# First gate product, weight sums, zero rows and residual loads moved in a one-core mixture kernel

## The chip, the cores and the metric

The kernel runs on one core of one Trainium2 chip. The time is the device time of one execution in microseconds (us), as the median of the runs shown.

## The reference

x has 32 sequences of 64 rows and 1024 columns in float32; taken together they are 2048 tokens. Two residual layers are computed:

```python
y = einsum('bct,bcd->bdt', x, W0[cond])            # a 64 x 64 matrix per sequence
x = x + y @ weight.T + lora(y, top-2 gates of y)    # 1024 -> 1024, 8 experts of rank 16
z = einsum('bsi,boi->bso', x, W1[adapter])          # a 1024 x 1024 matrix per sequence
gate, up = bitlinear(z, w_gate), bitlinear(z, w_up) # 1024 -> 2752
x = x + bitlinear(gate * up, w_down)                # 2752 -> 1024
# bitlinear(x, w): s = mean(|w|); q = round(clip(w / (s + 1e-5), -1, 1)); x @ (q * s).T
```

The three weights of the bitlinears are read once for the mean of their absolute values and again to be rounded to -1, 0 or 1.

## The kernel before

Every float32 operand of a product is split into a high and a low float16 part (act_t holds both for all tokens, 1024 columns on the partitions as 8 chunks). ScalarE writes the high part and VectorE the low part. The order of work on each engine is written out by hand; engines meet at semaphores (wait_ge), and an engine's instructions, the DMAs that it issues among them, go strictly in program order.

**First layer.** The 16 token tiles (NT) of 128 are mixed, gated and multiplied with the first weight; a tile's product is summed in PSUM pair t % 2 (pair[0] to pair[3] are 2-bank PSUM tensors of 1024 float32 columns), and VectorE's residual (L1566) adds x, which releases the pair (acc_released).

**Adapter products.** The sequences are sorted by adapter and paired into slots; there are between 16 and 20 slots, as the data decide, and the first 17 always have their instructions. linear (L854) is the product of a slot, 48 matmuls into pair k % 2. Its adapter rank and column are read into registers (slot_fields). copy_z takes the result out (ScalarE the left half, VectorE the right), linear_t transposes it on TensorE into pair 2 (L667), high_z (ScalarE) and low_z (VectorE) put it into act_t. The slots past FIRST_OPTIONAL = 17 stand in nested conditionals (optional).

Meanwhile GpSimd loads w_up and w_down in 24 pieces (load_piece, L631; six buffers), and VectorE sums the absolute values of each (sum_piece, L1621). The last four pieces are summed behind low_z of slot 12. When all are there, TensorE adds the sums over partitions in one product with ones (L922, into pair 3), and VectorE derives the clipping bounds and scales.

**Gate stage.** The 22 chunks (IC) of 128 inner columns go through a pipeline: load_q loads the natural rows of the three weights (SP queue), quantize (VectorE, L1656) clips them, round_q (ScalarE, L1202) rounds, turn_q (TensorE, L900) transposes, store_q (ScalarE, L1218) takes them into wa and wd, turn_a and turn_b (VectorE, L1679 to L1684, L1664 to L1669) form the sums of a seven-product (Strassen) scheme, which are stored to DRAM for later token groups (store_wa, store_wb). gate_up(n, s) (L946) is the product of chunk n with the first 512 tokens: 16 matmuls for the gate into pair 0, 16 for up into pair 1. scale_gate (ScalarE, L1235) and product (VectorE, L1700) multiply them; inter_sums (L1688 to L1693), high_inter (L1239) and low_inter (L1673) prepare the operand of the down stage. PE's order around its start is:

```python
            turn_q(1, 1, 0, (0, 1))
            linear_t(k - 2, 1)
            turn_q(1, 1, 0, (2,))
            optional(k, 1, pairs)
...
            gate_up(0, 0)
            pe.wait_ge(z_low, NSLOT)
            turn_q(2, 0, 1)
            gate_up(1, 1)
```

The last chunk has only 64 rows. VectorE waits until its tiles are free (q_turned), writes zeros into the other rows (L1653) and clips.

**Down stage and later token groups.** The tokens go in four groups of 512 (g = 0 to 3). down(g) (L1019) does seven products of 44 matmuls, each with one of seven weight sums, loaded into two alternating buffers by load_products (SP queue, L533; the load for product q waits until product q - 2 is done). The residual rows come by load_res (L545), four loads of 512 KB into the place of the inter sums st. From g = 1 on the gate and up products of a group come from the stored sums as well (unit, L982; loads L537), and GpSimd makes the low parts of the inter operand (L652) instead of VectorE. turn_t on VectorE (L1745 to L1756) prepares the next group's tokens during a down stage.

## Time and profile before

| what | value |
|---|---|
| median of 3 runs | 1394.69 us (1393.57 to 1394.8) |
| profiled execution, its own time | 1395.66 us |
| its span in the trace | 1394.0 us |
| TensorE busy (PE) | 1334.8 us, 96% |
| VectorE (DVE), ScalarE (ACT), GpSimd (POOL) busy | 54%, 27%, 11% |
| DMA | mean 223 GB/s |
| granted TensorE clock, mean | 0.986 of full |

The span is measured from the first to the last instruction of the profiled execution; its own time is 1.66 us longer. A matmul counts as busy with a modelled end, so two neighbouring rows overlap a little. In the rows, a bracket gives how long the engine was idle before the instruction and what released it; "issue" means that the trace shows nothing that it waited for. PEld is TensorE's weight load, SPq, ACTq and POOLq the queues of the engines that issue DMAs.

### The profile page before, as it was taken

To read this page: it belongs to the slowest core of one execution; us is meant where nothing else is said; L and a number is where in the kernel's file an instruction comes from. 1 tells how busy PE (TensorE), PEld (TensorE's weight loads), DVE (VectorE), ACT (ScalarE), POOL (GpSimd) and SP (SyncE) were. 2 spreads that over 40 slices of the span, in tenths; PEclk is the share of its full clock that TensorE was granted. 3 is DMA by queue.
4 is the path that set the end of the run, shared out by engine and by line. 5 is a ranking of instruction groups with operands and counts; after the bars stand their busy time and mean duration, and the time that the engine had idled before them with its cause. 6 is when DMAs were issued, how large, how long until landed. Compare 5 with 4: busy or idle time off the path is not lost.

```text
span 1394.0 us, 24489 instructions
## 1 busy us (share of the span) xinstructions
PE 1334.8 (96%) x8864; PEld 854.4 (61%) x8865; DVE 750.4 (54%) x1159; ACT 369.8 (27%) x401; POOL 157.5 (11%) x115
## 2 busy tenths in 40 slices
PE   5889899979999998999999999999999999999998
PEld 5874444434544454555544788854888844888843
DVE  4467555443355565888855355573455581455521
ACT  2423344100111145888730011120111110111100
POOL 3200000000111000000000122320133310222210
PEclk9999999989999999999999999999999999999999
DMA  8644999989997927999874644353634455544354
GB/s 211 161 137 176 337 408 416 331 261 221 295 265 236 271 95 265 360 350 358 291 264 166 219 159 149 139 202 138 228 141 153 148 194 185 204 158 155 128 196 143
DMA packets 174336, 310.67 MB, mean 223 GB/s; under 512 B 99360, under 2 KB 131360, under 8 KB 166464
## 3 DMA queue, kind: packets, MB, share of 16 engines
q1 hardware_dynamic: 158352, 254.04, 55.8%
q10 hardware_dynamic: 11440, 32.69, 6.2%
q0 software_dynamic: 4480, 23.07, 4.8%
q8 instruction: 41, 0.67, 0.2%
q14 instruction: 23, 0.19, 0.0%
HBM read 220.78 MB, written 68.03 MB: 207 GB/s over the span
## 4 chain that ended last, share of the span: by engine, by line
PE 73%; DMA 10%; DVE 5%; SPq 5%; issue 4%; ACT 2%; POOL 1%; POOLq 0%; ACTq 0%; DVEq 0%
PE pair L982 26%; PE pair L1019 15%; PE pair L854 12%; PE pair L946 10%; DMA region_q<-in_L_cond_weight 5%; PE pair L770 4%; DMA region_q<-wb_scratch 2%; PE pair L900 2%; DMA region_w<-in_L_ffn_w_gate 2%; SPq L474 2%; PE pair L737 1%; PE pair L667 1%; PE pair L725 1%; DMA region_q<-in_x 1%; SPq L445 1%
## 5 line engine op out<-in xcount | busy, mean ns | idle before, releaser
L982 PE MATMUL pair<-act_t,region_q 128*128 128x256 f16 x3696 | 404.0, 273 | 0.0
L982 PEld LDWEIGHTS pair<-act_t,region_q 128*128 128x128 f16 x3696 | 361.6, 98 | 42.5
L1019 PE MATMUL pair<-region_q,region_w 128*128 128x512 f16 x1232 | 267.6, 379 | 4.7 <-DMA region_q<-wb_scratch 4.4
L1019 PEld LDWEIGHTS pair<-region_q,region_w 128*128 128x128 f16 x1232 | 120.0, 98 | 151.0 <-DMA region_q<-wb_scratch 5.8
L652 POOL TENSOR_TENSOR region_w<-region_q,region_w 128x1792 f32 (+1 forms) x33 | 118.4, 3588 | 731.3 <-ACT region_w L1239 731.3
L854 PE MATMUL pair<-region_w,act_t 128*128 x816 | 178.9, 379 | 1.8 <-DVE region_q L1566 1.8
L770 PE MATMUL pair<-region_w,act_t 128*128 128x512 f16 x768 | 173.7, 384 | 0.0
L946 PE MATMUL pair<-act_t,region_q 128*128 128x512 f16 x704 | 158.5, 384 | 1.9 <-issue 1.9
L854 PEld LDWEIGHTS pair<-region_w,act_t 128*128 x816 | 79.9, 98 | 94.6 <-issue 2.3
L770 PEld LDWEIGHTS pair<-region_w,act_t 128*128 (+1 forms) x768 | 75.9, 99 | 89.1 <-issue 4.0
L1245 ACT ACTIVATE region_q<-pair 128x512 f32<-128x512 f32 x33 | 19.7, 597 | 403.3 <-PE pair L982 403.3
L946 PEld LDWEIGHTS pair<-act_t,region_q 128*128 128x128 f16 x704 | 68.8, 99 | 82.7 <-issue 6.3
L1339 DVE SCALAR_TENSOR_TENSOR act_t<-pair,act_t 128x512 f32 (+2 forms) x66 | 60.9, 946 | 91.9 <-ACT act_t L1052 86.9
L1239 ACT ACTIVATE region_w<-region_q 128x1792 f32 (+1 forms) x44 | 74.5, 1694 | 65.3 <-DVE region_q L1693 65.3
L1052 ACT ACTIVATE act_t<-pair 128x512 f32 (+2 forms) x66 | 51.3, 804 | 151.2 <-PE pair L667 100.5
L1767 DVE SCALAR_TENSOR_TENSOR region_q<-pair,out_c,region_q 128x512 f32<-128x512 f32 x32 | 24.0, 751 | 113.1 <-PE pair L1019 113.1
L1720 DVE TENSOR_TENSOR region_q<-pair,region_q 128x512 f32<-128x512 f32 x33 | 22.8, 692 | 90.1 <-PE pair L982 90.1
L667 PE MATMUL pair<-ident,region_q 128*128 128x128 f32 x328 | 48.3, 296 | 19.2 <-DVE region_q L1566 14.4
L1202 ACT ACTIVATE region_q<-region_q,inv 128x1024 f32<-128x1024 f32 x55 | 59.7, 1143 | 21.1 <-DVE region_q L1656 20.6
L1339 DVE SCALAR_TENSOR_TENSOR region_q<-region_q 128x1024 f16<-128x1024 f32 x41 | 49.5, 1222 | 27.8 <-ACT region_q L1052 27.7
L1218 ACT ACTIVATE region_q<-pair 128x1024 f16<-128x1024 int16 x66 | 63.8, 1022 | 2.4 <-PE pair L900 2.4
L1713 DVE TENSOR_TENSOR region_q<-pair,region_q 128x512 f32<-128x512 f32 x33 | 22.8, 692 | 74.9 <-PE pair L982 74.9
(185 smaller groups left out, 1021.6 us busy)
## 6 DMA issues: line engine op xcount, KB each, us to landing
region_q<-wa_scratch SPq DMA_DIRECT2D x33, 1792.0 KB, 7.3
region_q<-wb_scratch SPq DMA_DIRECT2D x28, 1408.0 KB, 6.0
region_q<-in_L_cond_weight SPq DMA_DIRECT2D x40, 512.0 KB, 8.9
w1s_scratch<-region_q ACTq DMA_DIRECT2D x40, 512.0 KB, 8.3
wa_scratch<-region_q SPq DMA_DIRECT2D x22, 896.0 KB, 6.4
region_q<-in_x SPq DMA_DIRECT2D x64, 256.0 KB, 4.9
region_w<-in_L_ffn_w_gate SPq DMA_DIRECT2D x16, 688.0 KB, 5.7
wb_scratch<-region_q SPq DMA_DIRECT2D x11, 896.0 KB, 4.2
```

What stands on the lines that cost most here:

```text
L652: pool.tensor_tensor(at(iop[:, 1], u), st[s][:, 0:7], at(iop[:, 0], u), ALU.subtract)\
L667: mm = pe.transpose(dst[:, k * P:(k + 1) * P], src[:, k * P:(k + 1) * P], idn[:, :])
L770: pe.matmul(pair[s][:, h * H:(h + 1) * H], act_t[:, a, k, ds(t * P, P)], w0_t[:, 4 * h:4 * h + 4, b, k, :], start=(k == 0 and a + b == 0), ...
L854: mm = pe.matmul(pair[s][:, h * H:(h + 1) * H], act_t[:, a, c, ds(at, P)], w1_t[:, ds(buf, 1), b, c, h * H:(h + 1) * H].rearrange("p x o - ...
L946: mm = pe.matmul(dst[:, s * H:(s + 1) * H], wa[s][:, first + k // 4, (k % 4) * P:(k % 4 + 1) * P], act_t[:, a, k, 0:GRP], start=(k == 0 an ...
L982: mm = pe.matmul(bank(s_bank, b)[:, (1 - h) * HALF:(2 - h) * HALF], ring_a[s][:, h, o_a, k], moving[a], start=(opens and h == 1 and k == 0 ...
L1019: mm = pe.matmul(bank(s_bank, b), iop[:, a, p, o_a, tp * P:(tp + 1) * P], ring_b[r][:, p], start=(opens and p == 0 and a == 0), stop=(not ...
L1052: return act.activation(dst, src, ACT.Copy, scale=scale)
L1202: act.activation(tile, tile, ACT.Copy, bias=ROUND, scale=inv[:, kind:kind + 1])\
L1218: act.activation(dst, src, ACT.Copy, bias=-BITS).then_inc(q_out[kind], 1)
L1239: act.activation(at(iop[:, 0], u), st[s][:, 0:7], ACT.Copy).then_inc(inter_high, 1)
L1339: return v.scalar_tensor_tensor(out=dst, in0=src, scalar=scale, in1=hi, op0=ALU.mult, op1=ALU.subtract)
```

## The change

On TensorE, gate_up(0, 0) is divided: the gate half goes ahead of the transposes of the last slot, and the up half behind them. That holds where no optional slot is in use (pairs <= k, tested in registers); otherwise the former order stands inside the other conditional. Slot 0's product waits for 15 released accumulators instead of 16. The register loads for slot k - 2 stand ahead of the wait for the sums instead of behind the mean product. ScalarE sums the last two weight pieces with Abs and an accumulated output; VectorE keeps the two before them. VectorE's turn_b(0) and turn_a(1, 1) go ahead of the last slot's low part, and quantize(3) behind it. The zeros of the last chunk are written by GpSimd. On the SP queue the load for the third product of each down stage goes ahead of the four residual loads.

```diff
--- before.py
+++ after.py
@@ -269,6 +269,7 @@
         w1_loaded = sem("w1_loaded")
         stat_loaded = [sem(f"stat_loaded{i}") for i in range(NBUF)]
         stat_done = sem("stat_done")
+        stat_done_a = sem("stat_done_a")
         gate_loaded = [sem(f"gate_loaded{i}") for i in range(2)]
         gate_summed = sem("gate_summed")
         stat_summed = sem("stat_summed")
@@ -566,8 +567,9 @@
                 if g == 0:
                     for h in range(2):
                         store_wa(sp, NP - 1, h, IC - 2 + h)
+                load_products(q0 + 2, STEPS[2][1])
                 load_res(g)
-                for j in range(2, 7):
+                for j in range(3, 7):
                     load_products(q0 + j, STEPS[j][1])
                 if g < NG - 1:
                     if g == 0:
@@ -647,6 +649,12 @@
                     load_piece(p)
 
 
+            for kind in range(3):
+                tile = (wq_gate[1], wq_up[1], wq_down[1])[kind]
+                pool.wait_ge(q_turned[kind], IC - 2)
+                wait_if(pool, zeroed, kind)
+                pool.memset(chunked(tile)[:, :, LAST:P] if kind == 2 else tile[LAST:P, :], 0.0).then_inc(zeroed, 1)
+
             def low_inter(g, u, s):
                 pool.wait_ge(inter_high, g * NP + u + 1)
                 pool.tensor_tensor(at(iop[:, 1], u), st[s][:, 0:7], at(iop[:, 0], u), ALU.subtract)\
@@ -842,7 +850,7 @@
                 rank, at = fields or slot_fields(k)
                 if isinstance(k, int) and k == 0:
                     pe.wait_ge(x1_low, 2)
-                    pe.wait_ge(acc_released, NT)
+                    pe.wait_ge(acc_released, NT - 1)
                 pe.wait_ge(w1_loaded, rank * 16 + 16)
                 wait_if(pe, z_copied_a, k - 1)
                 wait_if(pe, z_copied_v, k - 1)
@@ -901,6 +909,22 @@
                     mm.then_inc(q_turned[kind], 1)
 
 
+            def gate_part(n, s, dst, first):
+                pe.wait_ge(q_out[0], n + 1)
+                pe.wait_ge(q_out[1], n + 1)
+                wait_if(pe, prod_done, n - 1)
+                for k in range(KC):
+                    for a in range(2):
+                        mm = pe.matmul(dst[:, s * H:(s + 1) * H],
+                                       wa[s][:, first + k // 4, (k % 4) * P:(k % 4 + 1) * P],
+                                       act_t[:, a, k, 0:GRP],
+                                       start=(k == 0 and a == 0), stop=(k == KC - 1 and a == 1))
+                return mm
+
+            def gate_up(n, s):
+                gate_part(n, s, pair[0], 2)
+                gate_part(n, s, pair[1], 0).then_inc(gu_done, 1)
+
             def optional(k, s, pairs):
 
                 with pe.If(pairs > k):
@@ -918,9 +942,9 @@
 
             linear_t(k - 5, 0)
             linear(k - 3, 0)
+            fields = slot_fields(k - 2)
             pe.wait_ge(stat_summed, 2)
             pe.matmul(pair[3][:, 0:3], ones[:, :], ssum[:, 0:3], start=True, stop=True).then_inc(mean_done, 1)
-            fields = slot_fields(k - 2)
             linear_t(k - 4, 1)
             linear(k - 2, 1, fields)
             pairs = field(pe, F_CUM, NADP - 1, NSLOT)
@@ -932,22 +956,18 @@
             turn_q(1, 1, 0, (0, 1))
             linear_t(k - 2, 1)
             turn_q(1, 1, 0, (2,))
-            optional(k, 1, pairs)
-
-
-
-            def gate_up(n, s):
-                pe.wait_ge(q_out[0], n + 1)
-                pe.wait_ge(q_out[1], n + 1)
-                wait_if(pe, prod_done, n - 1)
-                for dst, first in ((pair[0], 2), (pair[1], 0)):
-                    for k in range(KC):
-                        for a in range(2):
-                            mm = pe.matmul(dst[:, s * H:(s + 1) * H],
-                                           wa[s][:, first + k // 4, (k % 4) * P:(k % 4 + 1) * P],
-                                           act_t[:, a, k, 0:GRP],
-                                           start=(k == 0 and a == 0), stop=(k == KC - 1 and a == 1))
-                mm.then_inc(gu_done, 1)
+            with pe.If(pairs > k):
+                linear(k, 1)
+                linear_t(k - 1, 0)
+                optional(k + 1, 0, pairs)
+                gate_up(0, 0)
+            with pe.If(pairs <= k):
+                pe.wait_ge(z_copied_a, k)
+                pe.wait_ge(z_copied_v, k)
+                gate_part(0, 0, pair[0], 2)
+                linear_t(k - 1, 0)
+                gate_part(0, 0, pair[1], 0).then_inc(gu_done, 1)
+
 
             def token_op(g, o, k):
 
@@ -1023,7 +1043,6 @@
                             if part[-1] == NP - 1:
                                 mm.then_inc(dn_done if tp == 0 else step_done, 1)
 
-            gate_up(0, 0)
             pe.wait_ge(z_low, NSLOT)
             turn_q(2, 0, 1)
             gate_up(1, 1)
@@ -1276,6 +1295,10 @@
             k = FIRST_OPTIONAL
             copy_z(k - 4, 1)
             high_z(k - 5)
+            for p in (NPIECE - 2, NPIECE - 1):
+                tile = stat_in[p % NBUF][:, 0:piece_size(p)]
+                act.wait_ge(stat_loaded[p % NBUF], 16 * (p // NBUF) + 16)
+                act.activation(tile, tile, ACT.Abs, accum_out=stat[:, p:p + 1]).then_inc(stat_done_a, 1)
             copy_z(k - 3, 0)
             for s in range(2):
                 act.wait_ge(x1_stored[s], 16 * NT // 2)
@@ -1648,9 +1671,6 @@
                 for kind in range(3):
                     tile = (wq_gate[h], wq_up[h], wq_down[h])[kind]
                     if last:
-                        v.wait_ge(q_turned[kind], n - 1)
-                        rest = chunked(tile)[:, :, LAST:P] if kind == 2 else tile[LAST:P, :]
-                        v.memset(rest, 0.0).then_inc(zeroed, 1)
                         v.wait_ge(zeroed, kind + 1)
                     v.wait_ge(wq_loaded[2 * kind + h], 16 * p + 16)
                     v.tensor_scalar(tile, tile, clip[:, kind:kind + 1], nclip[:, kind:kind + 1], ALU.min, ALU.max)                     .then_inc(clipped[kind], 1)
@@ -1808,9 +1828,10 @@
             k = FIRST_OPTIONAL
             copy_z(k - 4, 1)
             low_z(k - 5)
-            for p in range(NPIECE - 4, NPIECE):
+            for p in range(NPIECE - 4, NPIECE - 2):
                 sum_piece(p)
-            v.wait_ge(stat_done, NPIECE)
+            v.wait_ge(stat_done, NPIECE - 2)
+            v.wait_ge(stat_done_a, 2)
             v.tensor_reduce(ssum[:, 1:3], stat[:, :].rearrange("p (a b) -> p a b", a=2), X, ALU.add)\
                 .then_inc(stat_summed, 1)
             copy_z(k - 3, 0)
@@ -1839,10 +1860,10 @@
             quantize(2, 0, 1)
             copy_z(k - 1, 0)
             low_z(k - 2)
+            turn_b(0)
+            turn_a(1, 1)
             optional(k, 1, pairs)
             quantize(3, 1, 1)
-            turn_b(0)
-            turn_a(1, 1)
             for m in range(1, 4):
                 product(m - 1, (m - 1) % 2, (m - 1) // 2, (m - 1) // 2 % 2)
                 if m > 1:
```

## Rows read from the trace of the kernel before

**Rows 1.** Timeline ahead of slot 0: start us, us, engine, instruction [idle before <-releaser]

```profile
326.61 10.52 PE L854 MATMUL pair<-region_w,act_t 128*128 x48 [1.81 <-DVE region_q L1566]
```

**Rows 2.** Timeline around the mean product

```profile
478.25 1.14 POOL L631 DMA_DIRECT2D region_q<-in_L_ffn_w_down  x2 [0.31 <-issue]
...
486.85 7.96 DVE L1621 TENSOR_REDUCE stat<-region_q 128x1 f32<-128x1835 f32 x4
494.43 0.60 ACT L1052 ACTIVATE region_q<-pair 128x512 f32<-128x512 f32 x1 [8.96 <-PE pair L854]
...
495.07 0.39 PE L922 MATMUL pair<-ssum,ones 128*128 128x3 f32 x2 [0.68 <-DVE ssum L1814]
...
497.40 10.52 PE L854 MATMUL pair<-region_w,act_t 128*128 x48
```

**Rows 3.** Timeline around the first gate product

```profile
522.35 0.61 PE L900 MATMUL pair<-ident,region_q 128*128 128x128 f16 x8
...
525.71 1.14 PE L667 MATMUL pair<-ident,region_q 128*128 128x128 f32 x8 [2.75 <-DVE act_t L1339]
...
528.23 1.29 DVE L1339 SCALAR_TENSOR_TENSOR act_t<-pair,act_t 128x512 f32 x2 [2.67 <-ACT act_t L1052]
...
528.76 9.34 PE L946 MATMUL pair<-act_t,region_q 128*128 128x512 f16 x32 [1.90 <-issue]
...
531.05 3.23 ACT L1202 ACTIVATE region_q<-region_q,inv 128x1024 f32<-128x1024 f32 x3 [2.98 <-DVE region_q L1656]
...
538.13 0.69 ACT L1235 ACTIVATE region_q<-pair,inter_c 128x512 f32<-128x512 f32 x1 [3.86 <-PE pair L946]
```

**Rows 4.** Stretch: PE, PEld, DVE, ACT, POOL busy, PEclk, DMA, GB/s

```profile
526.00:533.00 7.00, 5.10 (x19) 2.06 (x17) 4.70 (x10) 3.04 (x4) 0.00 (x0) 0.54 0.58 200
```

**Rows 5.** Timeline around the last chunk of the gate stage

```profile
687.71 7.07 PE L946 MATMUL pair<-act_t,region_q 128*128 128x512 f16 x32
688.33 0.91 DVE L1653 MEMSET region_q<- 64x1024 f32 x1 [0.27 <-issue]
...
696.79 2.35 PE L900 MATMUL pair<-ident,region_q 128*128 128x128 f16 x24 [2.01 <-ACT region_q L1218]
...
705.35 0.83 SPq L533 DMA_DIRECT2D region_q<-wb_scratch  x2
...
713.60 46.57 PE L1019 MATMUL pair<-region_q,region_w 128*128 128x512 f16 x215
```

**Rows 6.** Chain that ended last: start us, us, what

```profile
670.04 1.34 PE pair L900 x24
...
925.24 9.68 DMA region_q<-wb_scratch
934.97 47.66 PE pair L1019 x220
```

**Rows 7.** TensorE's waits: us in total, times, longest us

```profile
PE pair L1019 <- DMA region_q<-wb_scratch: 4.4, 3, 1.9
```

**Rows 8.** The page's groups: busy us, mean ns, idle before

```profile
L854 PE MATMUL pair<-region_w,act_t 128*128 x816 | 178.9, 379 | 1.8 <-DVE region_q L1566 1.8
...
L1218 ACT ACTIVATE region_q<-pair 128x1024 f16<-128x1024 int16 x66 | 63.8, 1022 | 2.4 <-PE pair L900 2.4
```

**Rows 9.** DMA issues: KB each, median us to landing

```profile
region_q<-wb_scratch SPq DMA_DIRECT2D x28, 1408.0 KB, 6.0
...
region_q<-in_L_ffn_w_down POOLq DMA_DIRECT2D x1, 915.5 KB, 9.6
```

**Rows 10.** Timeline of GpSimd at the start

```profile
2.34 1.80 POOL L604 MEMSET region_w<- 128x2048 f32 x1
```

**Rows 11.** Timeline of the down stage g = 1

```profile
914.57 19.44 PE L1019 MATMUL pair<-region_q,region_w 128*128 128x512 f16 x88
...
919.84 3.58 POOL L652 TENSOR_TENSOR region_w<-region_q,region_w 128x1792 f16<-128x1792 f32 x1 [8.36 <-ACT region_w L1239]
920.00 3.70 DVE L1751 TENSOR_TENSOR region_q<-region_q 128x256 f32<-128x256 f32 x1
```

## Prediction, made before the changed kernel was run

> **What bounds the kernel now.** I read the page first: TensorE is the busy engine, and every other engine has slack on average, so only a gap on TensorE costs time. The second view is TensorE's list of waits; it is short, and the third view, the timeline around each wait, tells what each one is worth. Five places matter, and the five edits of the diff sit on them.
> (1) Ahead of the first adapter product TensorE stands 1.81 us for a VectorE instruction [rows 1].
> (2) Around the mean product: ScalarE picks up the finished slot at 494.43, so TensorE has ended there. VectorE is still adding four pieces (486.85, 7.96 us), the mean product comes at 495.07, and the next slot's product only at 497.40 [rows 2].
> (3) From the last turns of chunk 1 (ending 522.35 + 0.61 = 522.96) TensorE is idle 2.75 us until z can be transposed, then another 1.90 us that the trace calls issue, and the first gate product runs with a mean granted clock of 0.54 in its stretch: 32 matmuls in 9.34 us [rows 3, 4].
> (4) The last chunk's turn waits 2.01 us for ScalarE. Behind it VectorE writes zeros itself, 0.91 us and then two more, before clipping [rows 5].
> (5) In each later down stage the third load of step weights is issued at 925.24, behind four residual loads, and takes 9.68 us; three waits, 4.4 us in all [rows 6, 7].
> TensorE's pace, used below: 220 matmuls in 47.66 us, 0.2166 us each, so 6.93 us for 32 [rows 6].
>
> **The change part by part.**
> *Accumulator wait, NT - 1.* Slot 0's product writes pair 0, and token tile 15 was accumulated in pair 1, so the wait that ended at 326.61 goes: 1.81 us [rows 1]. The register loads for the slot come behind a long run of matmuls, where the sequencer is ahead; nothing replaces the wait. **1.8 us.** Bounds: 1.2 (some register time shows) and 1.8. The next adapter's weights have no wait in TensorE's list, so I cost the earlier need at nothing; if that cover were gone, the most that could be lost is the 1.8 itself.
>
> *Two sums to ScalarE, slot fields ahead of the wait.* VectorE keeps two of four sums, 7.96 / 2 = 3.98 us, ending about 490.8 rather than 494.8 [rows 2]. ScalarE has been idle 8.96 us before 494.43, that is from 485.47 [rows 2]. Its two pieces were issued by GpSimd from 478.25 over 1.14 us, and the very last one takes 9.6 us to land, so it is there by about 488.5 [rows 2, 9]. No row has an Abs with an accumulated sum; the nearest is ScalarE's pass over a tile of the loop (1.02 us for 1024 elements [rows 8]), which for 1835 gives some 1.8 us, and VectorE's own 1.99 us for the same piece is the upper end [rows 2]. The second ends near 490.5, four microseconds ahead of 494.4. So the mean product has its input early. What is left is the product itself, 0.39 us at most [rows 2], and eight transposes of about 0.9 us (1.14 with the clock down [rows 3]). Before: 497.40 - 494.4 - 0.9 = 2.1 us lost; after, 0.1 to 0.4. I take 0.2, because most of that 0.39 is latency. **1.9 us**, bounds 1.2 and 2.1. The Trainium skill ("ScalarE: Activation LUTs", Table sets) says that abs is in every table set, so that no table load comes with it; by its price of about 2.66 us for a switch the sum would still be the same, since ScalarE has the four microseconds. No row here shows such a load.
> Behind it the scales are ready some 0.4 us earlier while TensorE is 1.9 ahead. VectorE and ScalarE have idle time in front of the next slot's end, so I cost that at nothing; if gone, at most the 1.5 us difference comes back.
>
> *First gate product between the z transposes.* That this path runs is fixed by the data: 816 matmuls of L854 are 17 slots of 48, so pairs is 17 and the branch "pairs <= k" is taken [rows 8]. After 522.96 the skipped block costs something. The trace has one such skip, 1.90 us [rows 3]; with the second test I take the start as 525.0 (bounds: 523.0, all hidden, and 525.9, two us and more). The first half, 16 matmuls, is 3.47 us at full pace. Whether the clock has dropped by then is open: after 2.01 us of idle at place (4) it had, and from 696.79 on 1.34 (turns [rows 6]) + 13.86 (64 matmuls) should have led to 711.99, while the down product starts at 713.60: 1.6 us lost to the clock [rows 5]. The idle time here is as long, so I take 1.6: the first half ends at 530.1, transposes 1.0 (end 531.1), second half 3.47: 534.5. Before it ended at 538.1, where ScalarE starts [rows 3]. **3.6 us**, bounds 1.3 (late start and the 2.4 us that the clock took before, 9.34 - 6.93) and 5.6 (clock up and start at 524.6).
> What is late next: z_low. High part and low part follow the transposes in 528.23 + 1.29 - 526.85 = 2.67 us, so 533.8, under the second half. Then VectorE's clips of chunk 3, now behind it rather than ahead. ScalarE followed the first clip (529.5) at 531.05, so now at 535.4; rounding 3.23 (538.6), scale 0.69, three stores of 1.02 (542.3) [rows 3, 8]. TensorE wants chunk 3 after 534.5 + 1.34 + 6.93 = 542.8: a slack of 0.5 us where there were over 4. turn_b and turn_a of chunks 0 and 1 fill VectorE's idle time in front of z and only bring the stores on SP's queue forward.
>
> *Zero rows by GpSimd.* GpSimd has nothing queued between the last weight piece and stage g = 1, so its three waits hold up nobody. It can start when chunk 19's turns are done, over eight us before VectorE needs the zeros at 688.3. Its own memset of 2048 columns took 1.80 us [rows 10], so 0.9, 0.9 and 0.5 us. VectorE loses two waits and three memsets, 0.91 [rows 5] and by their sizes as much again and half of it, so some 2.3 us and the gaps, ahead of a TensorE idle of 2.01. The wait is gone, and with it the cold clock behind it. New start of the down stage: 687.71 + 6.93 + 1.34 + 13.86 = 709.8 against 713.60. **3.8 us.** The next to be late is the first down load, issued at 705.35 [rows 5] with 6.0 us to land [rows 9], 711.4. It depends on turn_b(10), which comes earlier by about 1.7 us (the product before it is released by TensorE at 694.6, not by ScalarE at 696.6): 709.7, just in time. Bounds 2.3 and 3.9.
> Against it speaks a row: a VectorE sum with two SBUF inputs, issued at 920.00, lasts 3.70 us and ends just behind GpSimd's instruction of 919.84 + 3.58 [rows 11]. If a memset holds VectorE in the same way, the four sums of inter_sums near 680 wait for up to 2.3 us. The Trainium skill ("GPSIMD Engine Reference", Key points) states that GpSimd shares its SBUF interfaces with VectorE and contends with instructions of two SBUF inputs; the trace agrees for the tensor_tensor, and no row here shows a memset beside such a sum. I take nothing, since a memset reads no input.
>
> *Residual rows behind the third load.* The third load waits for the first step, so 914.57 + 44 x 0.2166 = 924.1; it was issued at 925.24 behind four others. Alone in front it should take the median of 6.0 us [rows 9] and land at 930.2, ahead of 914.57 + 88 x 0.2166 = 933.6, when TensorE wants it (before: 934.97) [rows 6, 11]. The waits sum to 4.4 us [rows 7], and the modelled tail of the last matmul hides another 19.44 - 19.06 = 0.38 in each of three [rows 11]: **5.5 us**, bounds 3.0 (only the 1.1 us of earlier issue each) and 5.6. g = 0 had no wait. The four residual loads go out about 1 us later and land behind it, near 936; VectorE first reads them behind the third step's first half, 938.4 at the earliest. Cover gone would still cost little, since TensorE needs those sums two steps later.
>
> Sum: 1.8 + 1.9 + 3.6 + 3.8 + 5.5 = 16.6 us. The profiled execution took 1395.66 (span 1394.0) and would take 1379.1; the median of the three runs is 1.0 lower, 1394.69, so I forecast **1378.1**.
>
> **Rivals.**
> R1, the third load is late whatever its place: 9.68 us because the engines are full, not because of the order. For it: the DMA is well used in that stretch; against it: the 6.0 median in the same stage. Gain there 3.1: 1380.5. Chance 0.10.
> R2, the gate product gains little: branch and clock eat it, or chunk 3's rounding (slack 0.5) becomes the wait. Gain 1.0: 1380.7. Chance 0.17.
> R3, GpSimd's memsets hold VectorE's sums [rows 11]: 2.3 us, less about 0.9 of slack, 1.4 back: 1379.5. Chance 0.08. By the rule of the Trainium skill ("GPSIMD Engine Reference", Key points) this is the case if a memset counts as contending.
> R4, the clock stays up in the gate product: 1.6 more: 1376.5. Chance 0.12.
> R5, slower: TensorE pays the 1.90 us of a branch [rows 3] at loop ends, because code has moved. There are 9 passes of the gate loop and 3 x 4 of the unit loop. Nine payments cancel the gain, and all 21 give +40: 1418. Against it: no such issue time at any loop end now. Chance 0.02.
> R6, the change does not do what it says for most parts (gaps reappear at the next wait): gain 2 or less, 1393. Chance 0.03.
> Forecast: 0.48.
>
> **How the numbers follow.** The predicted time is the forecast's. The range takes R1 to R4 and two of the low bounds together: 1374.8 to 1383.3. A measurement here can tell about 0.2%, 2.8 us: faster 0.95 (all but R5 and R6), same 0.03, slower 0.02.
>
> **What would show it.** L854 starts without a wait at 324.8; the gap between the two slots around the mean product is under 1.5 us; 16 matmuls of the gate stand ahead of the last transposes at about 521 (525 less 3.7); chunk 21's turns have no wait; no TensorE wait on wb_scratch for g = 1 to 3. Wrong would be a wait for rounding at the third turn, VectorE sums of over 1 us beside a GpSimd memset, or a wait at the first down load.

## The result, and the profile after

The changed kernel took 1384.22 us (median of 4 runs, 1382.95 to 1385.14) against 1394.74 us for the kernel before beside it: a ratio of 0.9925, interval 0.9907 to 0.9942. It is faster by 10.5 us where 16.6 was forecast, and 1384.2 lies above the range, whose upper end was 1383.3. The profiled execution took 1384.71 us (span 1383.1, mean granted clock 0.988).

The page's groups for TensorE (line, engine, operation, count, busy and mean, then idle before and its releaser) show it at a glance:

```profile
L1002 PE MATMUL pair<-act_t,region_q 128*128 128x256 f16 x3696 | 404.1, 273 | 1.0 <-issue 1.0
...
L1039 PE MATMUL pair<-region_q,region_w 128*128 128x512 f16 x1232 | 267.1, 379 | 1.3 <-DMA region_q<-wb_scratch 1.0
...
L862 PE MATMUL pair<-region_w,act_t 128*128 x816 | 178.9, 379 | 0.0
...
L918 PE MATMUL pair<-act_t,region_q 128*128 128x512 f16 x704 | 158.0, 383 | 5.9 <-issue 5.9
```

The adapter products have lost their wait, and the later down stages no longer wait for weights (4.4 us [rows 7]). One wait has grown: ahead of the gate product TensorE stands 5.9 us for nothing that the timeline shows, where it stood 1.9 [rows 3]. And there are two new ones of 1.0 us each.

TensorE's timeline around the first gate product (start us, us, engine, instruction, idle before) answers to [rows 3]:

```profile
504.33 10.52 PE L862 MATMUL pair<-region_w,act_t 128*128 x48
...
516.54 0.61 PE L908 MATMUL pair<-ident,region_q 128*128 128x128 f16 x8
...
523.07 6.12 PE L918 MATMUL pair<-act_t,region_q 128*128 128x512 f16 x16 [5.92 <-issue]
529.02 1.04 PE L675 MATMUL pair<-ident,region_q 128*128 128x128 f32 x8
529.89 3.62 PE L918 MATMUL pair<-act_t,region_q 128*128 128x512 f16 x16
...
533.35 1.50 PE L908 MATMUL pair<-ident,region_q 128*128 128x128 f16 x24
```

Branches are not in the timeline, but the view of one source line has them (sequencer PEldq; duration in ns three times over, then the start). The branch of the new `pe.If(pairs > k)` lasts 6.1 us, and fills the gap; the last branch ahead of the gate product in the kernel before lasted 2.9. Here the changed kernel, then the kernel before:

```profile
L959 PEldq COMPARE_BRANCH  x1: 6094/6094/6094, 516.6 to 516.6; - x1
```

```profile
L909 PEldq COMPARE_BRANCH  x1: 2855/2855/2855, 525.7 to 525.7; - x1
```

The gate half is where the change puts it, but 5.92 us late, and then it runs cold (at a lowered clock): 6.12 us for 16 matmuls, against 3.62 for the 16 of the up half. In the view of stretches (PE, PEld, DVE, ACT and POOL busy, PEclk, DMA share, GB/s) the granted clock there is close to the lower of the two levels, 1.2 of 2.4 GHz:

```profile
523.00:529.00 6.00, 5.93 (x16) 2.21 (x17) 0.00 (x0) 0.00 (x0) 0.00 (x0) 0.57 1.02 397
530.00:534.00 4.00, 4.00 (x29) 2.12 (x27) 2.57 (x5) 1.08 (x2) 0.00 (x0) 1.00 0.02 7
```

The stretch around the mean product answers to [rows 2]:

```profile
483.00 1.73 ACT L1301 ACTIVATE region_q<-region_q 128x1835 f32<-128x1835 f32 x1 [1.24 <-DMA region_q<-in_L_ffn_w_down]
483.13 4.03 DVE L1644 TENSOR_REDUCE stat<-region_q 128x1 f32<-128x1835 f32 x2
484.64 0.19 ACT L1301 ACTIVATION_READ_ACCUMULATOR region_q<-region_q 128x1 f32 x1
...
487.19 0.18 DVE L1835 TENSOR_REDUCE ssum<-stat 128x2 f32<-128x24 f32 x1
490.52 0.28 PE L947 MATMUL pair<-ssum,ones 128*128 128x3 f32 x2
...
491.56 2.75 PE L862 MATMUL pair<-region_w,act_t 128*128 x12
```

The sums are ready at 487.4 and TensorE comes for them 3.1 us later. The last chunk of the gate stage and the first down product answer to [rows 5]:

```profile
674.66 2.66 POOL L656 MEMSET region_q<- 64x1024 f32 x3 [199.48 <-PE pair L908]
...
676.78 2.52 DVE L1676 TENSOR_SCALAR region_q<-region_q,clip,nclip 128x1024 f32<-128x1024 f32 x3
...
690.03 1.50 PE L908 MATMUL pair<-ident,region_q 128*128 128x128 f16 x24
...
694.98 0.37 SPq L384 DMA_DIRECT2D wb_scratch<-region_q  x1
...
700.39 0.83 SPq L534 DMA_DIRECT2D region_q<-wb_scratch  x2
...
706.36 0.82 PE L1039 MATMUL pair<-region_q,region_w 128*128 128x512 f16 x3 [1.01 <-DMA region_q<-wb_scratch]
```

The wait of 2.01 us ahead of the turns is gone and the 64 matmuls behind them run at full pace. The first down load is now the late one, by 1.01 us. In the later stages, the down stages of g = 1 and 2 have no row with a wait; inside the unit stage of g = 3 there is a new one:

```profile
907.34 66.93 PE L1039 MATMUL pair<-region_q,region_w 128*128 128x512 f16 x308
...
1299.64 11.53 PE L1002 MATMUL pair<-act_t,region_q 128*128 128x256 f16 x104 [0.98 <-issue]
1311.00 61.31 PE L1039 MATMUL pair<-region_q,region_w 128*128 128x512 f16 x282
```

**Where the time went.** Each line below is the difference of two starts on TensorE in one kernel less the same difference in another (positive: gained against the kernel before). The column "mended" is the last kernel of the experiments, e8.

| stage, from where to where | forecast | changed | mended |
|---|---|---|---|
| start to the last token tile's ones (323.34 before, 321.60, 321.89); no edit there | 0 | 1.74 | 1.45 |
| to slot 0's product (3.27 us before, 1.29, 1.30) | 1.8 | 1.98 | 1.97 |
| to the product behind the mean (170.79; 168.67; 168.67) | 1.9 | 2.12 | 2.12 |
| to the last slot's product | 0 | -0.03 | -0.14 |
| to chunk 2's turns (27.79; 29.02; 21.10) | 3.6 | **-1.23** | 6.69 |
| chunk 20's product to the first down product (25.89; 23.24; 22.05) | 3.8 | 2.65 | 3.84 |
| down stages, g = 1 (67.89; 66.76; 66.76) | | 1.13 | 1.13 |
| g = 2 (68.79; 66.76; 66.76) | | 2.03 | 2.03 |
| g = 3 to the end (73.77; 72.10; 72.07) | | 1.67 | 1.70 |
| the three together | 5.5 | 4.83 | 4.86 |
| unit stage of g = 3 (134.49; 135.65; 135.77) | 0 | -1.16 | -1.28 |
| sum | 16.6 | 10.9 | 19.5 |

The sums are the differences of the spans, 1394.0 less 1383.1 and less 1374.5. The 1.74 us at the start belongs to no edit: stages there differ from run to run by more, and in e6 below this part alone was some 4 us late. So the shares of the edits are read from stages, not from totals. Each stage is read from one execution of each kernel.

### The profile page after: what moved, and what is told of

It reads as the page before. It is cut to its first block, busy times and chain, and to the rows that moved or that the text cites. A ratio compares the mean times of both kernels' runs of the same rounds, so it can differ in the third digit from the quotient of the medians.

```text
span 1383.1 us, 24517 instructions
## 1 busy us (share of the span) xinstructions
PE 1331.9 (96%) x8864; PEld 853.0 (62%) x8865; DVE 744.2 (54%) x1154; ACT 372.8 (27%) x405; POOL 159.8 (12%) x118
## 4 chain that ended last, share of the span: by engine, by line
PE 77%; DMA 8%; SPq 4%; issue 4%; DVE 4%; ACT 1%; POOL 1%; POOLq 0%; DVEq 0%; ACTq 0%
PE pair L1002 27%; PE pair L1039 17%; PE pair L862 13%; PE pair L918 10%; DMA region_q<-in_L_cond_weight 5%; PE pair L778 4%; PE pair L908 2%; DMA region_w<-in_L_ffn_w_gate 2%; SPq L475 2%; PE pair L745 2%; PE pair L675 1%; PE pair L733 1%; DMA region_q<-in_x 1%; SPq L360 1%; ACT region_q L1071 1%
```

## The experiments

**e1: TensorE's old order in the changed kernel.** Everything else stays.

```diff
-            with pe.If(pairs > k):
...
-            with pe.If(pairs <= k):
...
-                gate_part(0, 0, pair[1], 0).then_inc(gu_done, 1)
+            optional(k, 1, pairs)
+            gate_up(0, 0)
```

> The changed kernel with TensorE's order of before around the first gate product (all other edits kept). Theory A (a taken conditional branch over more code costs TensorE more: 5.9 us of issue in the changed kernel against 1.9 in the kernel before): the two issue gaps are those of before (about 2 us in front of the gate product), the up half ends about 1.2 us earlier against the adapter products than in the changed kernel, and the time is 1 us lower, some 1383. Theory B (the 5.9 us are a wait for ScalarE's copy or store that the trace does not name): the gap of before stays at 1.9 us and the gate product starts after the same ScalarE instruction; then the time is that of the changed kernel or higher.

It took 1381.32 us (1379.65 to 1383.33, 4 runs), ratio 0.991, interval 0.988 to 0.994. Its timeline:

```profile
518.24 1.07 PE L675 MATMUL pair<-ident,region_q 128*128 128x128 f32 x8 [2.75 <-DVE act_t L1353]
521.56 9.67 PE L918 MATMUL pair<-act_t,region_q 128*128 128x512 f16 x32 [2.25 <-issue]
```

The 5.92 is 2.25 again, and from the last slot's product (502.67) to chunk 2's turns (531.07) it takes 28.40 us, 0.62 less than in the changed kernel. Two smaller waits left with it: the first down load is in time and the unit stages have no issue row. The two kernels' runs overlap a little (from 1382.95, up to 1383.33), but none of these numbers speaks for the new order.

**e2: the two conditionals exchanged,** the one that holds the gate half first, so that no skipped code lies between the turns and the gate half.

```diff
-            with pe.If(pairs > k):
-                linear(k, 1)
...
             with pe.If(pairs <= k):
...
+            with pe.If(pairs > k):
+                linear(k, 1)
```

> The changed kernel with the two conditionals in the other order: the gate half, the transposes and the up half first, behind them the code of the optional slots. Theory A: no gap over 1 us ahead of the gate half, since nothing is skipped there; the gap comes behind the up half instead, 4 to 6 us less what the queue of issued matmuls covers. Time 1378 to 1384. Theory B: the gap of 5.9 us stays in front of the gate half, time 1384.

It took 1379.36 us (1377.31 to 1381.83), ratio 0.9888, interval 0.986 to 0.9916.

```profile
518.00 3.62 PE L918 MATMUL pair<-act_t,region_q 128*128 128x512 f16 x16
...
528.44 2.00 PE L908 MATMUL pair<-ident,region_q 128*128 128x128 f16 x24 [2.50 <-DVE cnt L1667]
530.23 8.28 PE L918 MATMUL pair<-act_t,region_q 128*128 128x512 f16 x32
```

The gate half starts as the turns end (517.55 + 0.45) and at full pace. Now the skipped code lies behind the up half, which ends at 522.32 + 3.62 = 525.94, and chunk 2's turns come 2.50 us later. The trace puts that wait down to VectorE's count, behind z's low part. But the count was done at 527.57, 0.87 us before TensorE went on (in e3 and e4 it is 0.06), while the branch over the skipped code (L965) starts at 522.13 and lasts 6.14 us, to 528.27. The jump costs what it did; the up half, issued ahead of it, covers the rest. The clock has dropped by then: 32 matmuls take 8.28 us instead of 7.07. The stop is moved, and made smaller.

**e3: no conditional.** The code for slots 17 to 19 is left out on TensorE; the data use 17 slots, so the same work is done.

```diff
-            with pe.If(pairs > k):
-                linear(k, 1)
-                linear_t(k - 1, 0)
-                optional(k + 1, 0, pairs)
-                gate_up(0, 0)
-            with pe.If(pairs <= k):
-                pe.wait_ge(z_copied_a, k)
...
+            pe.wait_ge(z_copied_a, k)
...
```

> The changed kernel without the conditionals on TensorE: the code of the optional slots 17 to 19, which these inputs do not use, is left out, and gate half, transposes and up half stand in a row. Theory A: no gap at all, the gate half starts right behind the last turns and the clock stays up; against the changed kernel 5.9 + 2.7 us less, so 1375 to 1377. Theory B: a gap of several us stays, time within 1 us of 1384.

It took 1377.34 us (1374.75 to 1379.53), ratio 0.9879, interval 0.9848 to 0.9911.

```profile
516.46 3.62 PE L918 MATMUL pair<-act_t,region_q 128*128 128x512 f16 x16
...
526.05 1.51 PE L908 MATMUL pair<-ident,region_q 128*128 128x128 f16 x24 [1.65 <-DVE cnt L1661]
```

Without the branch the product has neither gap nor cold clock. From the last slot's product (503.80) to chunk 2's turns it is 22.25 us, so the edit is then worth 27.79 - 22.25 = 5.5 us, near its upper bound of 5.6. What is late next is z's low part: chunk 2's turns wait for VectorE's count. (This kernel has a stop of 1.14 us for issue in the unit stage of g = 1, where nothing was edited.)

**e4: the branch announced.** One comparison, and a mark ahead of the last slot's product tells TensorE's queue of the jump to come.

```diff
+            over = pe.mark_branch_hint_location()
             linear(k - 1, 0, fields)
...
-            with pe.If(pairs > k):
...
+            pe.br_lt(pairs, k + 1, on_true="gate_first", on_false="slots_first").branch_hint(over)
...
```

It took 1378.65 us (1377.75 to 1380.27), ratio 0.9891, interval 0.9862 to 0.9919.

```profile
517.15 3.61 PE L918 MATMUL pair<-act_t,region_q 128*128 128x512 f16 x16 [0.15 <-issue]
...
525.01 1.29 DVE L1368 SCALAR_TENSOR_TENSOR act_t<-pair,act_t 128x512 f32 x2 [2.23 <-issue]
...
526.41 1.51 PE L908 MATMUL pair<-ident,region_q 128*128 128x128 f16 x24 [1.25 <-DVE cnt L1673]
```

The kernel is as general as the changed one, with all slots' code in it, and the gap is 0.15 us; the branch itself lasts 0.47. The wait ahead of chunk 2 is named here: VectorE's low part stands 2.23 us for "issue" while ScalarE's high part, its input, has been there since 522.8. Ahead of it VectorE reads two registers for the slot, behind its test: the trace has the two loads with 0.90 and 0.76 us.

**e5 and e11: how much code is skipped.** e5 leaves out slots 18 and 19 of the skipped block on TensorE (one product and the gate product stay), e11 slot 19 alone. Neither slot is used by the data.

```diff
             with pe.If(pairs > k):
                 linear(k, 1)
                 linear_t(k - 1, 0)
-                optional(k + 1, 0, pairs)
+                linear(k + 1, 0)          # e11 only
+                linear_t(k, 1)            # e11 only
                 gate_up(0, 0)
```

> The changed kernel with the two adapter products of slots 18 and 19 (not used by these inputs) left out of the skipped block, so that the taken branch goes over one product and the gate code only. Theory A1 (the cost is a fetch of code that is far ahead): the gap ahead of the gate half falls from 5.9 us to 2 us or less. Theory A2 (the cost is the two comparisons and the branch, whatever the distance): the gap stays near 5.9 us.

> The changed kernel with a skipped block of two adapter products and the gate product (slot 19's code is left out, slot 18's stays), between the changed kernel (three products, issue gap 5.92) and e5 (one product, none). Theory L1 (each further piece of skipped code adds to the price): a gap between, 1.5 to 4 us, ahead of the first gate half. Theory L2 (a step: either the target has been fetched in time or it has not, and a fetch behind this place costs 5.8 to 6.1 whatever the distance): about 5.9 us, and the shorter 1.90 and 2.25 of the old order then come from the 2.75 us that TensorE stood in front of that branch, in which code was fetched already. Theory L3 (two products are still within reach): no gap above 0.3 us.

e5 took 1372.93 us and e11 1385.33 us, one run each. The first gate half of e5, and then of e11:

```profile
514.73 3.61 PE L918 MATMUL pair<-act_t,region_q 128*128 128x512 f16 x16 [0.30 <-ACT region_q L1236]
```

```profile
523.73 6.12 PE L918 MATMUL pair<-act_t,region_q 128*128 128x512 f16 x16 [6.00 <-issue]
```

With one product to jump over there is no gap (the branch lasts 0.48 us), with two it is 6.00 (6.17), with three 5.92 (6.09): a step, not a slope. My first idea, that each piece of skipped code adds to the price, falls. The two edits also shift all code behind them, and whether the length of the jump or the place where its target lies makes the step was not tested apart. (e11 has another stop, 2.12 us for issue in the last products of the gate stage, where nothing was edited.)

**e6: one comparison, not announced.** e4 without the mark, to part the announcement from the shorter test.

```diff
-            over = pe.mark_branch_hint_location()
...
-            pe.br_lt(pairs, k + 1, on_true="gate_first", on_false="slots_first").branch_hint(over)
+            pe.br_lt(pairs, k + 1, on_true="gate_first", on_false="slots_first")
```

> The kernel of the announced branch, with one comparison and the same taken branch, but not announced. Theory A1 (fetch): 4.5 to 6 us of gap, as in the changed kernel. Theory A2 (each test costs about 2 to 3 us): about 3 us.

It took 1389.99 us (one run; its start, which no edit touches, is some 4 us late, so only the stage counts):

```profile
528.14 6.31 PE L918 MATMUL pair<-act_t,region_q 128*128 128x512 f16 x16 [5.84 <-issue]
```

The gap is that of the changed kernel. So it is not the second test that costs (where both are run, in the changed kernel, the second lasts 0.08 us), and in e4 it was the announcement that helped.

**e7: the gate edit alone,** in the kernel before: TensorE's two conditionals and VectorE's turn_b(0), turn_a(1, 1) ahead of the last low part; none of the other edits.

```diff
+            with pe.If(pairs > k):
...
+            with pe.If(pairs <= k):
...
+                gate_part(0, 0, pair[0], 2)
+                linear_t(k - 1, 0)
+                gate_part(0, 0, pair[1], 0).then_inc(gu_done, 1)
-            optional(k, 1, pairs)
...
-            gate_up(0, 0)
```

> The kernel before with the first gate edit alone (TensorE's two conditionals, VectorE's turn_b and turn_a ahead of the last low part). Theory A: the gate product of chunk 0 ends about 1 us later against the adapter products than in the kernel before, so 1395 to 1397, ratio 1.000 to 1.0015. Rival (the loss comes only together with the other edits, because TensorE reaches the branch earlier): the gate product ends 2 us or more earlier than before, 1391 to 1393.

It took 1394.82 us (1390.5 to 1397.13, 12 runs) against 1394.08 (17 runs): ratio 1.0002, interval 0.999 to 1.0013. In its timeline:

```profile
526.08 5.66 PE L910 MATMUL pair<-act_t,region_q 128*128 128x512 f16 x16 [6.12 <-issue]
```

By itself the part that was to bring 3.6 us brings nothing. From the last slot's product (507.14) to chunk 2's turns (535.90) it takes 28.76 us, 0.97 more than in the kernel before, as expected. The rest of this execution, the fastest of the twelve, is worth a look, because two waits of the kernel before cost less in it. Behind the wait of 2.00 us at the last chunk the clock stays up:

```profile
694.75 1.50 PE L900 MATMUL pair<-ident,region_q 128*128 128x128 f16 x24 [2.00 <-ACT region_q L1228]
696.09 13.98 PE L910 MATMUL pair<-act_t,region_q 128*128 128x512 f16 x64
```

And with the old order of the residual loads TensorE waits 0.28, 0.21 and 0.59 us for the third loads, 1.1 together, where the kernel before had 4.4 [rows 7].

**e8: all mended.** e4, and on VectorE the register loads of the last slot's low part ahead of the one before it, and turn_b(10) ahead of the product in front of it, for the first down load.

```diff
+            last_fields = low_z_fields(k - 1)
...
-            optional(k, 1, pairs)
+            optional(k, 1, pairs, last_fields)
...
+                if m == IC - 2:
+                    turn_b(m // 2)
                 product(m - 1, (m - 1) % 2, (m - 1) // 2, (m - 1) // 2 % 2)
...
-                if m < IC and m % 2 == 0:
+                if m < IC - 2 and m % 2 == 0:
```

> The kernel of the announced branch, and in it VectorE's register loads for the last low part ahead of its wait, and turn_b(10) ahead of product(19). Theory: TensorE's wait on VectorE in front of chunk 2's turns (1.25 us) and its wait for the first down load (1.2 us) both go; against the announced branch alone 2 us less, 1375 to 1378, ratio to the kernel before 0.986 to 0.988. Rival (the first down load is late because its store and a code fetch run together, wherever turn_b stands): a wait of over 0.5 us stays at the first down product.

It took 1374.68 us (1373.71 to 1376.14, 4 runs) against 1394.08: ratio 0.9857, interval 0.9837 to 0.9878. This kernel beats both.

```profile
517.72 3.61 PE L918 MATMUL pair<-act_t,region_q 128*128 128x512 f16 x16 [0.16 <-ACT region_q L1243]
...
525.84 1.50 PE L908 MATMUL pair<-ident,region_q 128*128 128x128 f16 x24
...
697.67 27.57 PE L1045 MATMUL pair<-region_q,region_w 128*128 128x512 f16 x127
```

Neither chunk 2's turns nor the first down product waits. Left over is one stop of 1.12 us for issue in the unit stage of g = 3.

**e9 and e10: two parts undone in e8,** to price them without the others' side effects. e9 puts the residual loads ahead of the third load again; in e10 VectorE writes the zeros.

```diff
-                load_products(q0 + 2, STEPS[2][1])
                 load_res(g)
-                for j in range(3, 7):
+                for j in range(2, 7):
```

> The mended kernel (e8, 1374.68) with one part undone: the four residual loads ahead of the third load of step weights again. Theory E1 (the order alone made the waits): three waits of TensorE on wb_scratch come back in g = 1 to 3, about 1.5 us each by TensorE's own list and 4.9 us in the stages' lengths (67.9, 68.8 and 68.7 before), and the issue stall of 1.1 us in the unit stages stays, for it has nothing to do with these loads: 1379.6. Theory E2 (the stall in the unit stage is the price of the new order): it goes as well, so the loss is only 3.8: 1378.5, and no issue row above 0.5 us in a unit stage. Theory E3 (the third load is late for full engines, whatever its place): no change from 1374.7.

```diff
...
-                pool.memset(chunked(tile)[:, :, LAST:P] if kind == 2 else tile[LAST:P, :], 0.0).then_inc(zeroed, 1)
...
+                        v.wait_ge(q_turned[kind], n - 1)
+                        rest = chunked(tile)[:, :, LAST:P] if kind == 2 else tile[LAST:P, :]
+                        v.memset(rest, 0.0).then_inc(zeroed, 1)
```

> The mended kernel (e8, 1374.68) with one part undone: VectorE writes the zero rows of the last chunk itself, behind its two waits. Theory C1 (as the prediction costed it: the memsets and waits on VectorE and the cold clock behind the gap are the whole): chunk 21's turns wait about 2.0 us, the down product starts 3.7 us after where it would, 1378.4. Theory C2 (the first down load is the next to be late, and in e8 it had little room): as turn_b(10) is held by the zeros no more than before, the load is in time and the loss is the turns' wait of 2.0 us and some 0.9 us of clock: 1377.6. Theory C3 (the clips beside GpSimd's memsets pay back what was won): under 1 us of loss, 1375.5.

e9 took 1379.27 us (5 runs, ratio 0.9875, interval 0.985 to 0.9899), e10 1379.11 (6 runs, 0.9874, 0.9852 to 0.9897). Two of the rows of e9 that differ from e8:

```profile
921.01 47.66 PE L1044 MATMUL pair<-region_q,region_w 128*128 128x512 f16 x220 [1.28 <-DMA region_q<-wb_scratch]
...
1294.44 11.62 PE L1007 MATMUL pair<-act_t,region_q 128*128 128x256 f16 x105 [0.82 <-issue]
```

The three waits come back, 1.28, 0.49 and 1.24 us, 3.0 as listed and 3.7 by the stages (68.21 and 67.42 against 66.76 twice, and 20.68 against 19.06 in g = 3). The stop in the unit stage stays, so it is not the price of the new load order. And of e10:

```profile
686.86 1.95 PE L902 MATMUL pair<-ident,region_q 128*128 128x128 f16 x24 [2.00 <-ACT region_q L1237]
688.60 15.24 PE L912 MATMUL pair<-act_t,region_q 128*128 128x512 f16 x64
703.68 21.53 PE L1039 MATMUL pair<-region_q,region_w 128*128 128x512 f16 x99
```

From chunk 20's product (677.79) to the down product it is 25.89 us, exactly that of the kernel before, and 3.84 more than in e8: the wait, and the cold clock behind it. The ratios of e9 and e10 overlap with that of e8, and the executions shown are the slowest of their kernels, so these prices rest on the stages alone.

**e12: the branch announced late.** e8 with the mark moved behind the last slot's product.

```diff
-            over = pe.mark_branch_hint_location()
             linear(k - 1, 0, fields)
+            over = pe.mark_branch_hint_location()
             turn_q(1, 1, 0, (0, 1))
```

> The mended kernel with the branch announced later: the mark stands behind the last slot's product instead of ahead of it, so that only the 24 turns and 8 transposes, 2.3 to 2.5 us of TensorE's time, lie between the notice and the branch (in e8 12.8 us). Theory F1 (the fetch of the target's code takes 5.8 to 6.1 us from whatever starts it; in the old order 2.75 us of waiting and the transposes hid all but 1.90 of it): a gap of 3.3 to 3.7 us ahead of the first gate half. Theory F2 (the fetch is short once it is announced, and 5.9 is the price of finding out at the branch): a gap under 0.5 us, and the time of e8. Theory F3 (a notice so late is of no use): 5.9 us.

It took 1378.23 us, one run. The mark, the branch, and the timeline:

```profile
L956 PEldq BRANCH_PREFETCH_HINT  x1: 36/36/36, 512.7 to 512.7; - x1
```

```profile
L961 PEldq COMPARE_BRANCH  x1: 498/498/498, 518.5 to 518.5; - x1
```

```profile
519.22 3.61 PE L918 MATMUL pair<-act_t,region_q 128*128 128x512 f16 x16 [0.18 <-ACT region_q L1243]
...
523.54 0.81 PE L918 MATMUL pair<-act_t,region_q 128*128 128x512 f16 x3
525.07 2.98 PE L918 MATMUL pair<-act_t,region_q 128*128 128x512 f16 x13 [0.71 <-issue]
```

The gap is as small as in e8. But the notice was not 2.5 us: the mark ran at 512.7, while the slot's product, issued by then, kept TensorE busy until 516.7, and the branch came at 518.5. So the notice was 5.7 us, against 12.9 in e8, and 5.7 are enough. Three matmuls into the up half TensorE stops for 0.71 us, where e8 stops for 0.16; but e9 and e10, with the early mark of e8, stop for 0.28 and 0.44, so it isn't shown that the late mark does this. In all four an instruction packet starts 2.7 to 3.1 us behind the gate half's start; in e12 it took 1.87 us, in the others 0.93.

## Why the prediction failed, point by point

**The accumulator wait and the sums: right.** 1.98 and 2.12 us against 1.8 and 1.9. Each Abs took 1.73 us against the estimated 1.8, plus 0.19 for reading the accumulator, which no row of before had. ScalarE waited for its pieces, 1.24 and 0.40 us, and the sums were ready all the same. The 2.12 is the upper bound of 2.1. The remark on table loads holds: none stands at the Abs (the trace has three, the last at 119.3 us, as the kernel before has).

**The zeros by GpSimd: the price was right, the load behind them was not in time.** e10 against e8 gives 3.84 us for 3.8. In the changed kernel only 2.65 are left: the step that failed is "709.7, just in time", for TensorE waits 1.01 us for that load. The gain of turn_b(10) was right: its store goes out at 694.98, 6.29 us before that of the kernel before (701.27), of which the product of chunk 20 accounts for 687.71 - 683.12 = 4.59, and 1.70 are left. The load's 5.97 us were right too. But between them the store took 5.4 us instead of 4.1, a length that I had carried over unsaid. The price itself hangs on the clock: of two more executions with VectorE's zeros and the wait of 2.00 us, e10 has the clock down behind it (0.62 granted over the next 4 us, 0.57 in the kernel before), and e7 has it at 1.00 and loses the wait alone. R3, that the memsets hold VectorE's sums, is refuted: the two-input sums beside the memsets stay at 0.42 us. What stretched was the first of the three clips, with one tensor input, which ran beside the last memset: 1.08 us instead of 0.81, so 2.52 for the three instead of 2.25. The rule of the Trainium skill ("GPSIMD Engine Reference", Key points) speaks of instructions with two SBUF inputs, and also of those in a 2-port perf mode; beside a memset this trace shows no delay for the first kind, and whether the clips are of the second no run here shows.

**The residual rows: right in kind, a little large.** 4.83 us for 5.5, within the bounds. The three waits are gone, as forecast. The term was the waits plus a hidden tail of 0.38 in each; g = 1 gave 1.13, not its 0.96 + 0.38, and the tails were 0.12 to 0.18. The waits themselves differ from execution to execution: 4.4 us in the kernel before, 3.0 in e9 and 1.1 in e7, all with the old order. So 4.83 holds against the one execution that was profiled.

**The gate product: wrong, and this is the miss.** Without the 1.74 us at the start the edits brought 10.9 - 1.74 = 9.2 us of 16.6. Of the 7.4 that are missing 4.8 are here (3.6 against -1.23), 1.2 at the zeros, 1.2 in the unit stage of g = 3 and 0.7 at the residual rows; the first two terms gave 0.4 more. The step was "The trace has one such skip, 1.90 us [rows 3]; with the second test I take the start as 525.0". I read the price of a jump from its visible rest. In the kernel before, TensorE also needed 528.76 - 522.96 = 5.80 us from the end of the turns to the gate product; 2.75 of them were the wait for z and about 1.1 the transposes, and the 1.90 stood behind both. In e1 the same stretch takes 521.56 - 515.49 = 6.07. Where the branch follows the turns at once the whole shows: 5.92, 5.84, 6.00, 6.12 us in four kernels. The branches say it more plainly: 6.09, 6.16, 6.17 and 6.29 us in these four and 6.14 in e2, against 2.86 and 3.13 in the old order (before, e1). So the gate half began when it would have begun anyhow, after 5.9 us, and the transposes, formerly under that time, came on top of it. The clock term went the same way: TensorE idle for 5.9 us in a piece, then 6.12 us for 16 matmuls, where I had 3.47 and 1.6.

What the jump waits for is the code behind it. The evidence: no gap ahead of the gate half when the target is near (e5), when the code stands in line (e2, e3), or when the jump is announced (e4, e8, e12); the second test costs nothing (e6). The Trainium skill ("Runtime: NRT & Kernel Launch", Instruction fetch mechanics) says that an engine's code comes in blocks of 256 instructions, ahead of time only in sequence, and that a jump out of the two blocks at hand must wait for a transfer. The trace agrees in kind: within 517 to 523 the instruction queue moves one packet of 0.02 MB, and the price is a step between one and two skipped products. The presence of a packet proves little, since e5 moves one as well, behind the start of its gate half; its time says more. In the five kernels whose branch lasts over 6 us the packet starts 3.7 to 3.9 us behind the branch's start and takes 0.9 to 1.0, and the branch ends 2.4 us behind the packet's start. e3, without the branch, has no packet of this size between 508 and 528.

The same packet explains the 1.90 of the old order. In the kernel before it starts 3.9 us behind the first of two branches (L906, at 522.4) and 0.5 behind the second (L909); in e1 3.3 behind the first and just ahead of the second. So the transfer was under way before the second branch, within the 2.75 us of waiting: e1 shows it outright, the kernel before by its 0.5 us against 3.7 to 3.9. The "issue" row is the end of it. e12 does not speak against a fetch of some 6 us either, since its notice was 5.7. Three things stay open: that the packets are TensorE's, which the trace doesn't name and only their times suggest; what the first branch of the old order had to do with starting the transfer; and what fills the 3.7 us ahead of the packet.

R2 named the mechanism ("branch and clock eat it") and had 0.17; but it stopped at a gain of 1.0 for this part, and its total of 1380.7 still needed the full 3.8 of the zeros. R2's other half, chunk 3's rounding as the next wait, did not come: there is no wait at the third turn, in the mended kernel either. What came late next was z's low part, on VectorE, by the register loads ahead of it (e4, 1.25 us; with the loads moved, in e8, the wait is gone), which I had put safely under the up half.

**Code that moved.** R5 had TensorE pay for branches at loop ends. That did not happen, but a stop appeared inside the unit stage of g = 3, which the change doesn't touch: 0.98 us in the changed kernel, and 0.7 to 1.1 in e2, e4, e6 to e10 and e12. e3 has it in g = 1, e11 has 2.12 us in the gate stage, and the kernel before, e1 and e5 have none. e1 and e5 differ from the changed kernel in TensorE's code alone, and e7 has the old load order and VectorE's zeros; so it goes with the code on TensorE, and not with the load order (e9) or the zeros (e10). That it is a code block fetched late is argued, not shown. For it speaks that in all eleven kernels with such a stop an instruction packet starts 2.4 to 2.7 us before TensorE goes on; against a simple rule, that e1 has such a packet at the same place of the stage (1293.6) and no stop.

## What to carry to other kernels

What a jump in TensorE's stream costs can be hidden under a wait or under matmuls issued before it: the "issue" row shows only the part that nothing covers, and the duration of the branch, under its source line, shows more. Before work is moved ahead to just behind a branch, look at how far the branch jumps; keep the skipped block as short as e5's, put the common path in line, or announce the jump: 5.7 us of notice brought a gap of 5.9 us under 0.2. And when a stall goes away, follow the chain of store and load behind it with some slack: "just in time" was a microsecond late.

## What the hardware showed that was not expected

- The price of the jump is a step: a gap of 0.30 us or less over one adapter product and the gate product, 6.00 over two, 5.92 over three; the branch lasts 0.48, 6.17 and 6.09. An announced jump costs 0.15 to 0.18, its branch 0.37 to 0.50.
- TensorE's instructions are issued well ahead: in e2 the branch behind the up half starts at 522.13, when the half's 3.62 us of matmuls start at 522.32, and in e12 the mark behind the slot's product runs 4.0 us before the product ends.
- Idle time of 5.9 us is followed by 16 matmuls that take 6.12 us instead of 3.62, so the lower clock added 2.5 us to it. Behind 2.0 us of idle time the clock was down in the kernel before and in e10 and stayed up in e7.
- The last store of a weight sum (896 KB) took 4.1 us in the four kernels without an instruction packet in the 5.5 us from its issue (before, e1, e3, e5), and 5.4 to 5.7 in the five where one starts 0.8 to 2.5 us behind the issue (the changed kernel, e2, e4, e6, e7). Where the packet starts at 3.8 us or later (e8, e9, e10, e12) or at 0.1 (e11), the store took 4.1 to 4.6. So the two go together, and which is the cause was not tested.
- Abs with an accumulated output brings a second instruction of 0.19 us on ScalarE.
- A register load on VectorE for a dynamic address took 0.90 and 0.76 us in e4, right ahead of the instruction that needed it, and held it by 2.23 us in all.
